# A graph layer with a ternary feed-forward: the bias goes into the neighbour product through two rows of degrees

## The reference, cut to what matters

```python
def gnn(x, src, dst, W_self, W_neigh, b):            # 1250 nodes, 20000 edges, 512 features
    msg_sum = segment_sum(x[src], dst, 1250)
    deg = segment_sum(ones(20000), dst, 1250)
    neigh = msg_sum / maximum(deg, 1.0)[:, None]
    h = x @ W_self + neigh @ W_neigh + b
    h = where(h >= 0, h, 0.01 * h)
    return h / maximum(sqrt(sum(h * h, axis=1, keepdims=True)), 1e-12)

x = x + gnn(layernorm(x), src, dst, W_self, W_neigh, b)
x = x + ffn(layernorm(x))    # silu(x @ Wg.T) * (x @ Wu.T), then @ Wd.T; 1408 wide; each weight
                             # rounded to -s, 0 or s in groups of 128
```

## Time and profile before

| | |
|---|---|
| median of 3 runs | 337.06 us (336.26 to 338.64) |
| the profiled execution: its own time | 337.36 us |
| the profiled execution: its span | 335.6 us |
| PE busy | 315.7 us (94%) |
| DVE busy | 305.3 us (91%) |
| ACT busy | 236.9 us (71%) |
| POOL busy | 169.5 us (51%) |
| granted TensorE clock, mean | 0.997 |

### The profile page before, as it was taken

How to read it: one execution, slowest core, us unless ns; L and a number is a source line. 1 busy time by engine, 2 the same in 40 slices (tenths; PEclk the granted TensorE clock), 3 DMA queues, 4 the chain that set the end, 5 groups by cost and what they waited for, 6 DMA issues and landing times.

```text
span 335.6 us, 5723 instructions
## 1 busy us (share of the span) xinstructions
PE 315.7 (94%) x1521; PEld 237.5 (71%) x1521; DVE 305.3 (91%) x782; ACT 236.9 (71%) x636; POOL 169.5 (51%) x235
## 2 busy tenths in 40 slices
PE   7989999999999999789989999999999999999991
PEld 3434454444554787577858898998989988899981
DVE  3599999998996899997999999999999999999993
ACT  2178988689885666354897677867868688676760
POOL 6015100010100445600016686989889897899992
PEclk9999999999999999999999999999999999999998
DMA  7992322223330321100001111111110100000305
GB/s 216 288 225 69 94 57 71 65 63 94 98 87 27 103 82 48 27 14 0 1 17 25 24 28 26 27 25 28 25 25 21 22 2 1 2 1 1 114 11 183
DMA packets 23610, 19.62 MB, mean 58 GB/s; under 512 B 15230, under 2 KB 16084, under 8 KB 23576
## 3 DMA queue, kind: packets, MB, share of 16 engines
q1 hardware_dynamic: 23498, 19.16, 21.3%
q10 hardware_dynamic: 78, 0.08, 0.1%
HBM read 13.73 MB, written 2.56 MB: 49 GB/s over the span
## 4 chain that ended last, share of the span: by engine, by line
PE 58%; DVE 27%; issue 4%; ACT 3%; DMA 3%; POOL 2%; SPq 1%; DVEq 0%; ACTq 0%; POOLq 0%
PE bank L1481 43%; PE bank L1374 7%; DVE hot_dst L1138 5%; DVE tq_gu L1039 4%; DVE tq_d L1039 4%; PE bank L1418 4%; DMA x_sb<-in_x 3%; PE bank L1326 2%; DVE hot_src L1129 2%; DVE bn L1025 1%; DVE z L1175 1%; DVE z L1181 1%; DVE x_sb L1202 1%; PE bank L1315 1%; DVE bn L1208 1%
## 5 line engine op out<-in xcount | busy, mean ns | idle before, releaser
L1481 PE MATMUL bank<-x_hi,t_gu 128*128 128x376 f32 (+1 forms) x264 | 94.5, 358 | 1.6 <-DVE g_acc L1270 0.7
L1481 PE MATMUL bank<-x_lo,t_gu 128*128 128x376 f32 (+1 forms) x264 | 92.8, 351 | 0.0
L1374 PE MATMUL bank<-w_sb,xnT 128*125 128x512 f32 x160 | 82.9, 606 | 1.7 <-DMA w_sb<-in_L_gnn_W_neigh 1.3
L1270 DVE SCALAR_TENSOR_TENSOR g_acc<-bank,nscale,g_acc 128x376 f32<-128x376 f32 (+1 forms) x99 | 63.8, 644 | 3.7 <-PE bank L1481 3.3
L1270 DVE SCALAR_TENSOR_TENSOR u_acc<-bank,nscale,u_acc 128x376 f32<-128x376 f32 (+1 forms) x99 | 63.6, 643 | 0.0
L754 POOL TENSOR_TENSOR acc<-acc,d_one 128x376 f32<-128x376 f32 (+1 forms) x58 | 63.3, 1094 | 0.0
L764 POOL TENSOR_TENSOR hh<-sg,u_acc 128x376 f32<-128x376 f32 (+1 forms) x32 | 35.1, 1096 | 50.6 <-ACT sg L974 50.6
L693 POOL TENSOR_SCALAR thr<-absum 128x4 f32<-128x4 f32 (+1 forms) x34 | 9.7, 285 | 99.8 <-ACT mag_early L813 75.5
L1481 PEld LDWEIGHTS bank<-x_hi,t_gu 128*128 128x128 f32 x264 | 49.6, 188 | 7.9 <-DVE g_acc L1270 1.8
L1481 PEld LDWEIGHTS bank<-x_lo,t_gu 128*128 128x128 f32 x264 | 49.6, 188 | 3.3
L1326 PEld LDWEIGHTS bank<-hot_dst,hot_src 128*126 128x126 bf16 x157 | 20.6, 135 | 41.4 <-DVE hot_dst L1138 26.3
(11 more groups left out here) (143 smaller groups left out, 550.5 us busy)
## 6 DMA issues: line engine op xcount, KB each, us to landing
raw<-in_L_ffn_w_gate SPq DMA_DIRECT2D x11, 256.0 KB, 2.7
raw<-in_L_ffn_w_up SPq DMA_DIRECT2D x11, 256.0 KB, 2.6
out_x<-x_sb SPq DMA_DIRECT2D x10, 224.0 KB
raw<-in_L_ffn_w_down SPq DMA_DIRECT2D x8, 256.0 KB, 2.7
turned<-tq_gu SPq DMA_TRANSPOSE x80, 2.4
w_sb<-in_L_gnn_W_neigh SPq DMA_DIRECT2D x1, 1024.0 KB, 7.2
w_sb<-in_L_gnn_W_self SPq DMA_DIRECT2D x1, 1024.0 KB, 8.4
x_sb<-in_x SPq DMA_DIRECT2D x2, 448.0 KB
```

What stands on the lines that cost most here:

```text
L1270: nc.vector.scalar_tensor_tensor(out=to, in0=bank_of(u, what)[:, 0:w], scalar=nscale[:, j:j + 1], in1=to, op0=ALU.mult, op1=ALU.add).then_ ...
L1374: last = nc.tensor.matmul(to[0:TP, :], xnT[:, t, k * TP:(k + 1) * TP], w_sb[:, k, half * D:(half + 1) * D], start=k == 0, stop=k == KD - 1)
L1481: last = nc.tensor.matmul(bank_of(u, what)[:, 0:width(u)], w, parts[h], start=h == 0, stop=h == 1)
```

## The change

The bias of a node is its degree times the bias, over its degree. So the change lets PE add `deg * b` inside the neighbour product, where partition 125 of `a_t` and of `y_hi` and `y_lo` is free to carry one more term, and the product with `rdeg` makes `b` of it. (A node without an edge would have a degree of 0 there, where `rdeg` takes 1; the row therefore carries the degree after the maximum with 1, which DVE has in `rs`.)

- `bias` is loaded a second time, as eight rows of 128 numbers (`bias_s`). ACT rounds it (`bias_hi`), POOL takes the rest (`bias_lo`), and SP writes both into partition 125 of `y_hi` and `y_lo`, for source tiles 0 and 1.
- PE turns the column of degrees into rows (`turn_degrees`: once for tiles 0 to 5, in the middle of n = 0, once for tiles 6 to 9, in the middle of n = 4). DVE splits them (`degree_parts`, two instructions each time), and SP writes the two parts into partition 125 of `a_t`, for source tiles 0 and 1 (`degree_rows`, two DMAs each time). With two parts of the bias the four products of source tiles 0 and 1 add the whole of `deg * b`.
- The products of source tiles 0 and 1 have 126 rows in place of 125 and come last in each n, so that the rows may arrive while the other sixteen products run. Their number is the same.
- Tile 0 is done before the rows can be there. Its bias is still added by POOL, with one instruction, which now stands after the thresholds of load 6 in stage 1. The other nine additions are gone, and `neighbour_sum` waits for `z_out` in their place.
- DVE's two small instructions for the degrees of tiles 6 to 9 move from the end of n = 2 to the end of n = 1.

```diff
-    y_hi = place("y_hi", [TP, NT, D], F32R, "y")
-    y_lo = place("y_lo", [TP, NT, D], F32R, "y", NT * D * 4)
+    y_hi = place("y_hi", [TQ, NT, D], F32R, "y")
+    y_lo = place("y_lo", [TQ, NT, D], F32R, "y", NT * D * 4)
...
+            def degree_rows(i):
+
+                a, b = (0, DEG[1][1]) if i == 0 else DEG[2]
+                sp.wait_ge(deg_split, i + 1)
+                for s, part in enumerate((deg_hi, deg_lo)):
+                    sp.dma_start(a_t[TP:TQ, s, a * TP:b * TP].bitcast(F32).rearrange("o (n r) -> o n r", r=TP),
+                                 part[0:b - a, :].bitcast(F32)).then_inc(deg_rows[i], 16)
...
+                    for s in range(2):
+                        sp.dma_start(bias_s[s * BR:(s + 1) * BR, :], bias.rearrange("(c e) -> c e", e=P)).then_inc(bias_in2, 16)
...
+                if l == 12:
+                    sp.wait_ge(bias_split, 1)
+                    for y, part in ((y_hi, bias_hi), (y_lo, bias_lo)):
+                        sp.dma_start(y[TP:TQ, 0:2, :].bitcast(F32).rearrange("o s (c e) -> o (s c) e", e=P), part[:, :].bitcast(F32)).then_inc(bias_rows, 16)
...
+                if l == LOADS1 + RAWS + 2:
+                    degree_rows(0)
...
             for i, (_, f, down) in enumerate(by_dma):
+                if i == 1:
+                    degree_rows(1)
...
-            pool.wait_ge(bias_in, 16)
-            pool.wait_ge(joined, NB - 1)
...
-            for t in range(2):
-                add_bias(t)
+                if l == 6:
+                    pool.wait_ge(bias_in, 16)
+                    pool.wait_ge(z_out, 1)
+                    nc.gpsimd.tensor_tensor(z[:, 0, :], z[:, 0, :], bias_b[0:TP, :], ALU.add).then_inc(z_done, 1)
+                    pool.wait_ge(bias_high, 1)
+                    nc.gpsimd.tensor_tensor(bias_lo[:], bias_s[:], bias_hi[:].bitcast(F32), ALU.subtract).then_inc(bias_split, 1)
             for n in range(NT):
                 for l in down_loads_in(n):
                     scales_of(l)
-                if n + 2 < NT:
-                    add_bias(n + 2)
...
+                if slot == 20:
+                    act.wait_ge(bias_in2, 32)
+                    nc.scalar.activation(bias_hi[:], bias_s[:], ACT.Copy).then_inc(bias_high, 1)
...
+            def degree_parts(i):
+
+                n = DEG[1][1] if i == 0 else DEG[2][1] - DEG[2][0]
+                dve.wait_ge(deg_turned, i + 1)
+                if i:
+                    dve.wait_ge(deg_rows[0], 32)
+                else:
+                    dve.wait_ge(z_done, 1)
+                nc.vector.tensor_copy(deg_hi[0:n, :], bank[7][0:n, 0:TP]).then_inc(deg_high, 1)
+                dve.wait_ge(deg_high, i + 1)
+                nc.vector.tensor_tensor(deg_lo[0:n, :], bank[7][0:n, 0:TP], deg_hi[0:n, :].bitcast(F32),
+                                        ALU.subtract).then_inc(deg_split, 1)
+
             inverse_degrees(0, DEG[1][1], 2, 0)
+            dve.wait_ge(bias_rows, 32)
             for j in mid_jobs:
+                if j == load_end[LOADS1 + 1]:
+                    degree_parts(0)
                 ternary_of(j)
...
                 dve.wait_ge(n_ready, t + 1)
-                dve.wait_ge(z_done, t + 1)
+                if t:
+                    dve.wait_ge(z_out, t + 1)
+                else:
+                    dve.wait_ge(z_done, 1)
...
+                if n == 1:
+                    inverse_degrees(DEG[2][0], DEG[2][1], 3, 2)
                 if n == 2:
-                    inverse_degrees(DEG[2][0], DEG[2][1], 3, 2)
+                    degree_parts(1)
...
+            def turn_degrees(a, b, step):
+
+                pe.wait_ge(rdeg_done, step + 1)
+                nc.tensor.transpose(bank[7][0:b - a, 0:TP], rs[0:TP, a:b], ident[0:TP, 0:TP]).then_inc(deg_turned, 1)
+
...
-                for s in range(NT):
+                for i in range(NT):
+                    s = (i + 2) % NT
+                    rows = TQ if s < 2 and n else TP
                     if n == 0:
                         pe.wait_ge(ylo_done, s + 1)
-                    if s == 3 and n >= 4:
+                    if s == 0 and n == 1:
+                        pe.wait_ge(bias_rows, 32)
+                        pe.wait_ge(deg_rows[0], 32)
+                    if s == 0 and n == DEG[2][0]:
+                        pe.wait_ge(deg_rows[1], 32)
+                    if i == 3 and n >= 4:
                         transpose_x1(n - 4)
                     for y in (y_hi, y_lo):
-                        last = nc.tensor.matmul(bank[4 + n % 2][0:TP, :], a_t[0:TP, s, n * TP:(n + 1) * TP], y[:, s, :],
-                                                start=s == 0 and y is y_hi, stop=s == NT - 1 and y is y_lo)
+                        last = nc.tensor.matmul(bank[4 + n % 2][0:TP, :], a_t[0:rows, s, n * TP:(n + 1) * TP], y[0:rows, s, :],
+                                                start=i == 0 and y is y_hi, stop=i == NT - 1 and y is y_lo)
+                    if i == 4 and n == 0:
+                        turn_degrees(0, DEG[1][1], 0)
+                    if i == 2 and n == 4:
+                        turn_degrees(DEG[2][0], DEG[2][1], 2)
```

More of the change, by code:

```diff
@@ L139, in gnn_ffn @@
     assert offs[0] + 2 * wide[0] <= 6656 and offs[-1] + 2 * wide[-1] <= KD * F * 2
+    BR = D // P
+    spare = 2 * (2 * F + 8 * P)
+    bias_s = place("bias_s", [2 * BR, P], F32, "tq_d", spare)
+    bias_hi = place("bias_hi", [2 * BR, P], F32R, "tq_d", spare + P * 4)
+    bias_lo = place("bias_lo", [2 * BR, P], F32R, "tq_d", spare + 2 * P * 4)
+    assert spare + 3 * P * 4 <= 9472 and offs[0] + 2 * wide[0] <= spare
     row19, row20, row21 = (i * D * 2 for i in (19, 20, 21))
@@ L190, in gnn_ffn @@
     flag = small("flag", [P, 1], I32)
+    bias_home = used["small"]
     bias_b = small("bias_b", [P, D], F32)
+    deg_hi, deg_lo = (place(f"deg_part{s}", [DEG[1][1], TP], F32R, "small", bias_home + s * P * 4) for s in range(2))
     absum = small("absum", [P, 132], F32)
@@ L246, in gnn_ffn @@
         z_done = sem("z_done")
+        bias_in2 = sem("bias_in2")
+        bias_high = sem("bias_high")
+        bias_split = sem("bias_split")
+        bias_rows = sem("bias_rows")
+        deg_turned = sem("deg_turned")
+        deg_high = sem("deg_high")
+        deg_split = sem("deg_split")
+        deg_rows = [sem(f"deg_rows{i}") for i in range(2)]
         src_wide = sem("src_wide")
@@ L728, in _ @@
                     check_windows(l)
-            pool.wait_ge(bias_in, 16)
-            pool.wait_ge(joined, NB - 1)
-            def add_bias(t):
-                pool.wait_ge(z_out, t + 1)
-                nc.gpsimd.tensor_tensor(z[:, t, :], z[:, t, :], bias_b[0:TP, :], ALU.add).then_inc(z_done, 1)
-            for t in range(2):
-                add_bias(t)
+                if l == 6:
[4 more added lines that the diff above has]
+                    nc.gpsimd.tensor_tensor(bias_lo[:], bias_s[:], bias_hi[:].bitcast(F32), ALU.subtract).then_inc(bias_split, 1)
             for n in range(NT):
@@ L843, in _ @@
                     act.wait_ge(y_ready, t + 1)
-                    nc.scalar.activation(y_hi[:, t, :], bank[4 + t % 2][0:TP, :], ACT.Copy).then_inc(yhi_done, 1)
+                    nc.scalar.activation(y_hi[0:TP, t, :], bank[4 + t % 2][0:TP, :], ACT.Copy).then_inc(yhi_done, 1)
                 if i == 2 and 1 <= t <= NT:
@@ L1121, in _ @@
                         dve.wait_ge(ternary, load_end[LOADS1 - 1])
-                    nc.vector.tensor_tensor(y_lo[:, t - 1, :], bank[4 + (t - 1) % 2][0:TP, :],
-                                            y_hi[:, t - 1, :].bitcast(F32), ALU.subtract).then_inc(ylo_done, 1)
+                    nc.vector.tensor_tensor(y_lo[0:TP, t - 1, :], bank[4 + (t - 1) % 2][0:TP, :],
+                                            y_hi[0:TP, t - 1, :].bitcast(F32), ALU.subtract).then_inc(ylo_done, 1)
                 if slot < SLOTS:
```

## The result

| | before | changed |
|---|---|---|
| median | 337.32 us (8 runs, 336.26 to 340.38) | 334.02 us (8 runs, 333.06 to 334.68) |
| ratio, 95% interval | | 0.9905 (0.9878 to 0.9931) |
| span of the profiled execution | 335.6 us | 332.8 us |
| PE, DVE, POOL busy | 315.7, 305.3, 169.5 us | 316.4, 301.1, 157.4 us |

What follows compares the result with a forecast made beforehand. It took POOL's additions to hold DVE in stage 2, making PE wait for xn. A stage 2 gain of 3.3 us less 1.2 us lost in stage 1 took 337.06 to 335.0 us, range 333.2 to 336.9.

Steps and rivals of the forecast that it cites:

- What bounds the kernel: Stage 2: POOL's additions hold DVE's two-operand instructions, so PE waits three times for xn: 0.63, 1.93 and 1.13 us.
- The ceiling: Stage 2 can win at most PE's three waits for xn, 3.69 us; less 0.4 for two turns, 3.3 us.
- Part 1: Stage 2: without the additions DVE loses its excess, together 6.3 us, more than PE's 3.69 us of waits.
- Part 2: Added on PE: two turned columns at 0.2 us each, 0.4 us in all; products of 126 rows cost nothing.
- Part 3: DVE in stage 2: new waits for PE, yet xn in time, with 0.8 us spare at tile 1, 1.2 at tile 2.
- Part 4: DMAs of the degree rows in stage 2 land before PE asks for them, so they are hidden.
- Part 5: Stage 1: POOL's addition near 44.5 us holds a DVE instruction, costing 1.2 us (0 to 1.7) that stays lost.
- The sum: Whole kernel: -3.3 us from stage 2 and +1.2 us in stage 1 make -2.1 us, so 335.0 us.
- the hidden case: Rival: stage 1 hides its delay, leaving stage 2's gain alone, 333.8 us; chance 0.2.
- stay late in stage 2: Rival: DVE's second split waits longer, xn of tiles 1 and 2 late by 0.7 us each, 336.4 us; chance 0.14.
- late degree rows: Rival: PE waits before the last four products of n = 1 for the rows' DMA, perhaps 345 us; chance 0.05.
- other cause: Rival: DVE's long instructions in stage 2 don't come from the additions, so nothing is gained, 338.5 us; chance 0.04.

Runs made afterwards that it cites:

- e2: Changed kernel plus nine pairs of unused half-width additions (125 x 256) on POOL in stage 2; 335.28 us, ratio 0.9955, stage 2 52.13 us.
- e3: Changed kernel plus unused POOL memsets in stage 2, four at each of nine places, writing SBUF and reading nothing; 334.16 us, ratio 0.9918, stage 2 50.68 us.
- e5: Changed kernel plus ten unused full-size POOL additions at the old places, reading one tile twice; 337.10 us, ratio 1.0015, stage 2 53.30 us.
- e9: Changed kernel plus ten unused full-size POOL additions at the old places, reading two different tiles; 339.07 us (one run), stage 2 55.15 us.
- e6: Changed kernel without the rows of degrees, their turns, splits and DMAs, so tiles 1 to 9 get no bias; 334.2 us (one run), stage 2 50.48 us.
- e4: Kernel before with its ten POOL additions moved, eight to the end of stage 1, two behind stage 2's last thresholds; 342.49 us, ratio 1.0178.

## Why the prediction came out as it did

- **What bounds the kernel** was right: additions hold DVE, DVE is late with `xn`, PE waits. e2, e3, e5 and e9 show each link.
- **The ceiling** of 3.69 us was a little low, and with it the net of 3.3. The gain up to the third transposition was 35.60 - 31.54 = 4.06. The bracketed waits count from the modelled end of the last product, and that reaches past the moment at which the next could start. PE before the third wait, kernel before:

```profile
142.10 0.39 PE L1418 MATMUL bank<-y_hi,a_t 125*125 125x512 f32 x1
142.32 0.40 PE L1418 MATMUL bank<-y_lo,a_t 125*125 125x512 f32 x1
```

  Products follow each other every 0.23 us and are shown 0.40 long. From 142.32 + 0.23 to the transposition at 143.85 are 1.30 us, where the bracket says 1.13. The other two waits come to 0.79 and 2.10 in the same way, together 4.19.
- **Part 1** was right in kind and size; the groups fell to 2.09, 2.19 and 0.87 us for my 1.94, 2.20 and 0.88.
- **Part 2**: a turn shows 0.1 us in the chain, not 0.2, and e6 puts the two together at 0.2 us at most.
- **Part 3**: DVE's waits came at the three places, 0.39, 0.53 and 0.52 us for my 0.6, 0.25 and 0.7. The spare time I had too high. For tile 1 I had 0.8 us, counted to the latest start of `xn` (0.96 before PE asks); it started 0.90 before, so nothing was left. Counted from the first product PE came 0.57 us earlier than I had it (26.44 for 27.01), since its waits had been longer than I took them for and its two turns cost less, and `xn` 0.29 later (25.54 for 25.25). That PE did not wait here was a matter of a tenth of a microsecond, and not what my sum had promised.
- **Part 4** was right: the rows went out at 113.1 and 134.2 us (I had 113.1 and 134.5, with the later start), and PE didn't wait.
- **Part 5** was right: 1.29 us for my 1.2. That it "stays lost" held, for here the delay was not taken up anywhere in 63 us. The block was caught, not `hot_src`; `bias_lo` caught a `hot_dst`, which I had not thought of as one that can be held, for 0.18 us where I had 0.1. The term bias_hi at nothing held: it took 0.29 us, and ACT's idle time behind it fell from 0.57 to 0.41 us.
- **The sum** by these: -4.1 + 1.3 = -2.8, as the spans have it. My -2.1 missed that by 0.7: 0.8 from the ceiling and the turns, less 0.1 from stage 1. The other 0.3 of the 1.0 us by which the median of 334.02 lies below my 335.0 is no more than rounds of one kernel differ by (the kernel before has medians of 337.32, 336.52 and 336.56 in three sets of rounds).
- **The range** has a slip at its lower end: the hidden case with turns at 0.1 is 337.06 - (3.69 - 0.2) = 333.6, not 333.2. The measured time lies inside either way.

Of the rivals, a stage 1 that hides its delay gives 333.8, nearer to the measured median than my own number, but its mechanism is refuted: stage 1 did lose 1.29 us. DVE did not stay late in stage 2, though with nothing to spare at tile 1. The late degree rows and the other cause did not appear either.

## What to carry to other kernels

Read a GpSimd operation that reads SBUF as a lock of its own length on VectorE's instructions with two SBUF operands (and on such as `hot_dst`), and place it by VectorE's idle stretches, not by its own due time: the same addition cost stage 1 of this kernel 1.3 us at 44 us and 0.9 at 99 us, both with the small `bias_lo` behind it, and at 103 us nothing of its own. Never string several together beside work that VectorE must finish. And take what a wait costs PE from start to start of its products, not from the modelled idle time.

## What I had not expected of the hardware

- `hot_dst` (TENSOR_SCALAR, 16-bit numbers, one SBUF input) is held like the instructions with two inputs: 1.31 us where it takes 0.26.
- POOL's addition of 125 x 512 takes 1.04 us when both operands and the output are the same 512 columns (e5), and 1.27 when the second operand is other columns (e9) or another tile.
- An operation on only 8 partitions and 128 columns (`bias_lo`) held DVE as well, a `hot_dst` for 0.18 us, and took 0.50 to 0.76 us on POOL.
- In e4 PE was busy for 2.99 us of the 5 from 100 us on, at a granted clock of 1.00, and for 1.18 us of the next 5, at 0.76; from 110 to 115 us, back at work, it had 0.55, nearer to the lower of its two levels (1.2 GHz) than to the upper.
